# Ternary weights transposed by DMA, level scores without a rounded split, and new instruction lists in a one-core level tower

## The reference

```python
h = level_emb[levels] * 0.15
h = h + attention(layernorm(h))        # 16 query heads, 4 key heads of 16, softmax over all 128 tokens
def _quantize(W):                      # W1: 1024 x 256, W2: 256 x 1024
    gamma = jnp.mean(jnp.abs(W))
    return jnp.clip(jnp.round(W / (gamma + EPS)), -1.0, 1.0)
h = h + relu(layernorm(h) @ _quantize(W1).T + b1) @ _quantize(W2).T + b2
```

## Time and profile before

| | us |
|---|---|
| median of 3 runs (lowest, highest) | 53.73 (53.23, 56.08) |
| the profiled execution: time | 54.04 |
| the profiled execution: span | 52.0 |
| PE busy | 45.6 (88%) |
| PE weight loads | 36.3 (70%) |
| DVE busy | 38.0 (73%) |
| ACT busy | 34.2 (66%) |
| POOL busy | 15.7 (30%) |

### The profile page before, as it was taken

The page is one execution under the profiler, slowest core; times in us unless marked ns, Lnnn a source line. Parts: engine busy times, 40 slices in busy tenths (PEclk is TensorE's granted clock), DMA queues, the critical chain, the costliest instruction groups (busy, mean ns, idle before and its releaser), DMA issues.

```text
span 52.0 us, 1206 instructions
## 1 busy us (share of the span) xinstructions
PE 45.6 (88%) x394; PEld 36.3 (70%) x394; DVE 38.0 (73%) x141; ACT 34.2 (66%) x77; POOL 15.7 (30%) x37
## 2 busy tenths in 40 slices
PE   0999999999999799999999999999999999993000
PEld 0336469894758688768679999989999798860000
DVE  3558994698985289999999996269858889659100
ACT  0083231380799997989988999999967793509000
POOL 5689952000005950009200579970000000000000
PEclk9999999999999999999999999999999999999997
DMA  0183919999753100000000000000000005555893
GB/s 0 36 234 77 44 63 350 410 432 368 198 124 98 47 7 0 0 0 0 0 0 13 0 0 0 0 6 0 0 0 0 0 13 200 203 208 195 295 385 127
DMA packets 4658, 5.37 MB, mean 103 GB/s; under 512 B 1117, under 2 KB 4141, under 8 KB 4653
## 3 DMA queue, kind: packets, MB, share of 16 engines
q1 hardware_dynamic: 4312, 5.02, 31.2%
q10 hardware_dynamic: 341, 0.29, 1.6%
HBM read 3.21 MB, written 2.10 MB: 102 GB/s over the span
## 4 chain that ended last, share of the span: by engine, by line
PE 76%; DVE 10%; POOL 3%; issue 1%; ACT 1%; DVEq 1%
PE pswt L1258 16%; PE psmisc L1273 15%; PE psg L1067 8%; PE psg L1063 5%; PE psg L1194 4%; POOL rs L445 3%; PE psg L1240 3%; DVE aw L952 2%; PE psg L1106 2%; PE psg L1153 2%; PE psg L1203 2%; PE psg L1154 2%; PE psg L1158 2%; DVE cn L892 2%; DVE hq L906 2%; DVE st L910 2%
## 5 line engine op out<-in xcount | busy, mean ns | idle before, releaser
L587 ACT ACTIVATE hr<-pswt,b1c 128x256 f32<-128x256 f32 x16 | 7.6, 484 | 1.2 <-PE pswt L1258 0.9
L1273 PE MATMUL psmisc<-w2T,hh 128*128 128x256 f32 x32 | 8.2, 285 | 0.0
L1273 PE MATMUL psmisc<-w2T,hl 128*128 128x256 f32 x32 | 8.1, 281 | 0.0
L937 DVE TENSOR_TENSOR hl<-hr,hh 128x256 fp32r<-128x256 f32 x16 | 6.7, 435 | 1.2 <-ACT hh L589 0.9
L1258 PE MATMUL pswt<-xhi,w1T 128*128 128x256 f32 x32 | 7.0, 299 | 0.0
L1258 PE MATMUL pswt<-xlo,w1T 128*128 128x256 f32 x32 | 6.4, 280 | 0.0
L1273 PEld LDWEIGHTS psmisc<-w2T,hh 128*128 128x128 f32 x32 | 6.0, 189 | 0.1
L1273 PEld LDWEIGHTS psmisc<-w2T,hl 128*128 128x128 f32 x32 | 6.0, 189 | 0.0
L445 POOL TENSOR_TENSOR rs<-ve,mhalf 128x1 f32<-128x1 f32 x4 | 2.7, 686 | 9.1 <-DVE ve L918 9.1
L440 POOL TENSOR_TENSOR voc<-vo,cpos 128x272 f32<-128x272 f32 x4 | 2.7, 714 | 8.1 <-DVE cpos L858 8.1
L1258 PEld LDWEIGHTS pswt<-xhi,w1T 128*128 128x128 f32 x32 | 4.9, 189 | 0.3
(11 more groups left out here) (177 smaller groups left out, 108.4 us busy)
## 6 DMA issues: line engine op xcount, KB each, us to landing
w<-in_L_ffn_W_dram SPq DMA_DIRECT2D x4, 512.0 KB, 6.8
out_dram<-aw SPq DMA_DIRECT2D x7, 256.0 KB, 2.4
wq<-in_L_attn_Wq_dram SPq DMA_DIRECT2D x1, 256.0 KB, 3.5
wo<-in_L_attn_Wo_dram SPq DMA_DIRECT2D x4, 64.0 KB
out_dram<-aw ACTq DMA_DIRECT2D x1, 256.0 KB, 2.9
emb<-in_L_tok_level_emb_dram SPq DMA_DIRECT2D x1, 128.0 KB
bo_bc<-in_L_attn_bo_dram SPq DMA_DIRECT2D x1, 128.0 KB, 8.8
b_bc<-in_L_ffn_b_dram SPq DMA_DIRECT2D x1, 128.0 KB, 7.3
```

What stands on the lines that cost most here:

```text
L587: nc.scalar.activation(hr[:, n % NHR, :], pswt[n % 2][:, 0:RH], ACT.Relu, bias=b1c[:, j:j + 1]).then_inc(a_hr, 1)
L937: V.tensor_tensor(hl[:, n, :], hr[:, n % NHR, :], hh[:, n, :].bitcast(F32), ALU.subtract).then_inc(v_hl, 1)
L1273: ins = mm(psmisc[r][:, 0:D], part[:, n, r * P:(r + 1) * P], w2T[:, j, :], start=(j == 0 and m == 0), stop=(j == FC - 1 and m == 1))
```

## The change

- **DMA-transposed weights.** Both matrices are made ternary in the same way on ACT (`rounded(w, i)`, `ternary(w, i)` for w = 0, 1). SP issues four DMA transposes of a 128 x 1024 bf16 half each, one per finished `ternary`. POOL copies the result in eight pieces of 128 x 512 from bf16 to the matmul's type (`weights_in`). PE's `weights_t`, ACT's `weights_out`, DVE's `signs` and `ternary` and the two bf16 identities are gone. The sums of absolute values of W2 move from ACT to DVE (a reduction over 1024 columns, twice).
- **Scores.** No split: keys and queries stay f32, the 64 rows of a head pair go into 64 partitions twice, so that matmuls use half of the array's rows. Groups 0 and 1 get one f32 matmul of 512 columns each, with the lower and with the upper 64 rows. Groups 2 and 3 get none: PE writes only mask and maximum, and DVE adds the score table `st` (`arguments`, 128 x 512, PSUM to SBUF) before ACT's exp. The masks are four matmuls of 32 rows.
- **Loads.** W1 is loaded third, by rows of 1 KB; `wk`, `wv`, `bk` go to the ACT queue, and the tokens come in three DMAs. `b1` is gathered element by element.
- **Stores.** ACT copies sequences 0 and 2 of a group, DVE 1 and 3; a pair's store waits for one copy of each.
- **Lists.** All five lists are written anew.

```diff
-            sp.dma_start(b1c[:], b1.rearrange("(p j) -> p j", j=FC)).then_inc(d_b1, 16)
+            sp.dma_start(b1c[:], b1.rearrange("(j p) -> p j", p=P), allow_slow_non_contiguous=True).then_inc(d_b1, 16)
             sp.dma_start(b2_bc[:], ...)
+            for w in range(2):
+                for i in range(2):
+                    sp.wait_ge(a_tern, 2 * w + i + 1)
+                    sp.dma_start_transpose(wT[:, w, FC * i:FC * i + FC, :], tern[:, w, 1024 * i:1024 * i + 1024]).then_inc(d_wt[2 * w + i], 16)
...
+            def weights_in(u):                                  # POOL
+                w, q = divmod(u, FC // 2)
+                pool.wait_ge(d_wt[u // 2], 16)
+                src = wT[:, w, 4 * q:4 * q + 4, :].rearrange("p (j k) f -> p j k f", k=KC)
+                if w == 0:
+                    nc.gpsimd.tensor_copy(w1T[:, 2 * q:2 * q + 2], src).then_inc(g_wt, 1)
+                else:
+                    nc.gpsimd.tensor_copy(w2T[:, 2 * q:2 * q + 2, :].rearrange("p j (k f) -> p j k f", k=KC), src).then_inc(g_wt, 1)
...
             inverse_root(0)                                     # POOL's list
             inverse_root(1)
+            weights_in(0)
+            weights_in(1)
+            weights_in(2)
+            weights_in(3)
+            weights_in(4)
             inverse_root(2)
+            scaled_mean(2)
+            weights_in(5)
             inverse_root(3)
-            scaled_mean(2)
             scaled_mean(3)
-            residual(0)
             residual(1)
+            weights_in(6)
             residual(2)
+            weights_in(7)
             residual(3)
...
             exps(0)                                             # ACT's list, from the first exp on
             exps(1)
             exps(2)
-            rounded(0)
+            rounded(0, 0)
+            rounded(0, 1)
             ctx_out(0)
             ctx_out(1)
             exps(3)
-            rounded(1)
-            ternary(0)
+            ternary(0, 0)
+            ternary(0, 1)
             ctx_out(2)
-            ternary(1)
-            weights_out(0)
+            rounded(1, 0)
+            ternary(1, 0)
             ctx_out(3)
             x_hi(0)
-            weights_out(1)
             x_hi(1)
-            weights_out(2)
-            weights_out(3)
-            weights_out(4)
+            rounded(1, 1)
             hidden(0, 0)
             hidden(0, 1)
-            weights_out(5)
+            ternary(1, 1)
             hidden(0, 2)
...
+            def query_out(i):                                   # DVE; ACT has the other half of the columns
+                dve.wait_ge(p_q, 1)
+                V.tensor_copy(qs[64 * i:64 * i + 64, :].rearrange("p (a e l) -> p a e l", a=2, e=2)[:, :, 1, :],
+                              psg[3][64:P, 0:2 * L].rearrange("p (a l) -> p a l", a=2)).then_inc(v_q, 1)
+            def arguments(g):                                   # DVE, groups 2 and 3
+                dve.wait_ge(p_et, 1)
+                dve.wait_ge(a_st, 1)
+                V.tensor_tensor(et[:, g], st[:].unsqueeze(1).to_broadcast([P, BG, P]), psg[g][:, :].rearrange("p (b n) -> p b n", b=BG),
+                                ALU.add).then_inc(v_arg, 1)
+            def magnitudes(i):                                  # DVE
+                dve.wait_ge(d_w2[i], 16)
+                V.tensor_reduce(asum[:, 2 + i:3 + i], w2[:, i, :], AX_X, ALU.add, apply_absolute_value=True).then_inc(v_abs, 1)
...
-            def scores_t(g):
-                rhs = qs[:].unsqueeze(1).to_broadcast([P, BG, P])
-                mm(psg[g][:, :], khi[:], rhs, start=True, stop=False)
-                mm(psg[g][:, :], klo[:], rhs, start=False, stop=False)
-                mm(psg[g][:, :], gone[:], seln[:, g * BG:(g + 1) * BG]..., start=False, stop=True)
+            def scores_t(*gs):
+                for g in gs:
+                    h = slice(64 * (g % 2), 64 * (g % 2) + 64)
+                    mm(psg[g][:, :], ktm[h, :], qs[h, :].unsqueeze(1).to_broadcast([64, BG, P]), start=True, stop=False, skip_group_check=True)
+            def masks():
+                for g in range(NG):
+                    q = slice(L * g, L * (g + 1))
+                    mm(psg[g][:, :], gone[q, :], seln[q, :].unsqueeze(2).to_broadcast([L, BG, P]), start=g in SUBTRACTED, ...)
...
             queries()                                           # PE's list, up to the first context
-            keep_warm(5, psg[0])
             values()
             scores()
-            scores_t(0)
-            levels_out()
+            score_table()
+            scores_t(0, 1)
             level_ends()
             prefix_t()
-            scores_t(1)
+            keep_warm(4, psg[3])
+            counts()
+            keep_warm(1, psg[3])
             maxima()
-            scores_t(2)
-            scores_t(3)
-            counts()
+            masks()
+            keep_warm(4, psmisc[0])
             less_max()
```

More of the change, by code:

```diff
@@ L293, in level_tower @@
         a_abs = sem("a_abs")
-        v_sgn = sem("v_sgn")
+        v_abs = sem("v_abs")
         p_gam = [sem(f"p_gam{i}") for i in range(2)]
         v_thr = sem("v_thr")
-        v_tern = sem("v_tern")
-        p_wt = sem("p_wt")
-        a_wt = sem("a_wt")
+        d_wt = [sem(f"d_wt_{i}") for i in range(4)]
+        g_wt = sem("g_wt")
         p_f1 = sem("p_f1")
@@ L524, in max_hi @@
                 nc.scalar.activation(mhi[:], psmisc[1][:, 0:P], ACT.Copy).then_inc(a_mhi, 1)
[L526 to L533, removed]
-                act.wait_ge(c_magic, 2)
-                c = slice(1024 * q, 1024 * q + 1024)
-                src = w1[:].rearrange("p j d -> p (j d)")[:, c]
-                nc.scalar.activation(aw[:, 0, c], src, ACT.Identity, bias=magic[:, 0:1], scale=inv[:, 0:1]).then_inc(a_rnd, 1)
@@ new lines, in rounded @@
+            def rounded(w, i):
+                if w == 0:
+                    act.wait_ge(a_abs, 2)
+                act.wait_ge(v_inv, w + 1)
+                act.wait_ge(c_magic, 2)
+                js = slice(FC // 2 * i, FC // 2 * (i + 1))
+                y = aw[:, w, 1024 * i:1024 * i + 1024]
+                if w == 0:
+                    nc.scalar.activation(y, w1[:, js, :].rearrange("p j d -> p (j d)"), ACT.Identity,
+                                         bias=magic[:, 0:1], scale=inv[:, 0:1]).then_inc(a_rnd, 1)
+                else:
+                    nc.scalar.activation(y.rearrange("p (j k f) -> p j k f", k=KC, f=P),
+                                         w2[:].rearrange("p k (j f) -> p j k f", f=P)[:, js], ACT.Identity,
+                                         bias=magic[:, 0:1], scale=inv[:, 1:2]).then_inc(a_rnd, 1)
@@ L974, in _ @@
[L974 to L989 removed]
+            spread_selectors()
+            level_scan()
+            level_ends()
+            end_codes()
@@ L990, in _ @@
+            key_blocks()
+            end_columns()
+            level_onehot(0)
+            query_out(0)
+            query_out(1)
+            level_onehot(1)
+            prefix_max(0)
+            values()
+            count_blocks()
+            prefix_max(1)
+            mask_selectors()
+            top_onehot()
+            gone_levels()
+            low_rows()
+            counts_out()
             max_parts()
-            count_blocks()
-            counts_out()
-            signs(1)
+            arguments(2)
@@ L994, in _ @@
             threshold(0)
+            arguments(3)
             inverse_sums(0)
+            table_bias()
+            inverse_sums(1)
             normalise(0)
-            inverse_sums(1)
             normalise(1)
+            magnitudes(0)
+            magnitudes(1)
             inverse_sums(2)
+            add_table(0)
             normalise(2)
-            table_bias()
+            row_stats(0)
             threshold(1)
-            ternary(0)
-            add_table(0)
-            row_stats(0)
+            row_moments(0)
@@ L1006, in _ @@
             add_table(1)
-            row_moments(0)
+            variance_eps(0)
             row_stats(1)
             inverse_sums(3)
-            variance_eps(0)
             row_moments(1)
+            variance_eps(1)
+            norm_rows(0)
             normalise(3)
-            variance_eps(1)
-            ternary(1)
-            norm_rows(0)
             norm_rows(1)
-            ternary(2)
-            ternary(3)
+            add_table(2)
             x_lo(0)
             x_lo(1)
-            add_table(2)
+            row_stats(2)
```

406 lines of the change are left out of this document (167 added, 239 removed).

## The result

| | before | changed kernel |
|---|---|---|
| median of the runs | 53.68 us (53.23 to 56.08, 4 runs) | 61.05 us (60.42 to 61.95, 4 runs) |
| ratio, 95% interval | 1 | 1.1283 [1.1183, 1.1383] |
| profiled execution: time, span, mean granted clock | 54.04, 52.0, 0.995 | 60.42, 58.5, 0.89 |

What follows compares the result with a forecast made beforehand. ScalarE's list, with TensorE and VectorE close behind, sets the FFN's start, and TensorE runs the FFN. Profiled 54.04 - 0.1 (up to the last spread) - 0.2 (tail) = 53.7, or 53.4 us on the median's scale; range 52.0 to 55.8.

Steps and rivals of the forecast that it cites:

- the front: Stretch up to the first exp: queries 0.9 later, scores 0.35 later, yet first exp at 16.3, a gain of 0.5.
- the condition: Front: the forecast is wrong if queries or tokens come over 0.5 us later than predicted, since nothing behind recovers it.
- First exp: End of the front: starts at 16.3 instead of 16.83, a gain of 0.5, with less_max near 15.5 instead of 15.81.
- First exp to FFN: ScalarE's list up to x_hi(1) grows from 9.76 to 10.75; FFN starts at 27.7 instead of 28.00, gain 0.3.
- Transposes: Weight transposes by DMA before POOL's copies: each lands after 3.0 us, bounds 2.4 and 6.8.
- rivals 2 and 4: FFN: transposes land late (55.0 us at 5 us each, chance 0.19) or queue up (68 to 69 us, chance 0.04).
- rival 2: FFN's first half: transposes land late, the third delaying ffn2(0, 0); 55.0 us if 5 us each; chance 0.19.
- POOL copies: Copies of transposed weights on POOL: 0.75 us per 128 x 512 piece, bounds 0.4 and 2.0.
- rival 3: POOL copies cost 1.2 us a piece, so ffn1(1, 0) moves by 2: 55.4 us; chance 0.09.
- First half of the FFN: ffn1(1, 0) at 35.95, 0.85 later, TensorE idling 1.1 us; twelve ffn2 done instead of eight, worth 0.95.
- rival 1: FFN's first half: the 1.1 us of idle TensorE are not there, so 52.3 us; chance 0.30.
- Tail: Last stores: the pair before the last is ready 0.4 earlier; gain 0.2, bounds 0 and 0.4.

Runs made afterwards that it cites:

- e1: The changed kernel, all of it, but with both load lists of the kernel before: 54.18 us, ratio 1.0107.
- e7: e1 with ctx_out(0), ctx_out(1) and exps(3) ahead of rounded(0, 1) on ScalarE, and table_bias and W2's second sum later on VectorE: 54.33 us, ratio 1.0115.
- e9: e1 without the twelve filler matmuls between table_t and the queries: 54.67 us, ratio 1.0128.
- e6: The changed kernel with 25 fillers instead of 3 where TensorE waits for bq: 61.15 us.
- e8: e1 with all four groups' scores written by TensorE, none added on VectorE, and five fillers left out: 54.17 us, ratio 1.0082.
- e3: The changed kernel with W1 issued on SP only when bk has landed, bv standing behind that wait: 58.01 us, ratio 1.0814.
- e5: As e3, but with bv issued ahead of SP's wait for bk: 58.29 us, ratio 1.0806.
- e4: The kernel before with the change's two new load lists and nothing else: 63.03 us, ratio 1.1785.
- e2: The changed kernel with bk and bq issued ahead of wk and wv on ScalarE's queue: 64.95 us, ratio 1.2086.

## Why the prediction was wrong, step by step

**The step that failed.** It is the front: "which also wait for the second weight copy on ScalarE, behind seven DMA issues instead of two: queries end near 10.75". I priced the issues and never the landings. I let the small loads land as they did before while 2 MB were issued ahead of or beside them, and the early issue of W1 does not stand in the sum at all. The queries ended at 14.63. With the loads of before they end at 10.15 in e1 and 10.67 in e7, at or ahead of my figure, so the rest of the step was sound. I named the condition myself: the forecast is wrong "if queries or tokens come over 0.5 us later than I have them". Tokens came 1.8 later than before (5.90 against 4.12), and I gave the condition no price and no rival.

The price was in the trace of before. Its DMA issues hold three small loads that are issued behind the weights:

```profile
bo_bc<-in_L_attn_bo_dram SPq DMA_DIRECT2D x1, 128.0 KB, 8.8
b_bc<-in_L_ffn_b_dram SPq DMA_DIRECT2D x1, 128.0 KB, 7.3
...
b1c<-in_L_ffn_b_dram SPq DMA_DIRECT2D x1, 4.0 KB, 7.6
```

A 4 KB load lands after 7.6 us there, and 64 KB issued ahead of the weights after 3.2. As an estimate, those rows bound the landing of a small load between 3 and 8.8 us, and by the dear end `bq`, issued at 3.31, comes at 12.1. Its matmul stood at 8.40 before, so that is 3.7 us on the chain and a rival at 57.1, the clock not yet counted.

**The clock, which no term held.** I had all stretches at full clock, because the trace of before shows nothing else. Of the 7.41 us, 2.14 and 2.20 are work of TensorE at half clock. The second amount came again in e9, with the loads in time (2.08); the first was not measured apart. The fillers that the change adds stand before and behind the wait for `bq` and not in it.

**First exp.** Predicted 16.3; with the loads as before 15.80 in e1 and 16.34 in e7, whose lists are the same up to there: a gain of 1.03 and of 0.49 where I said 0.5. `less_max` starts at 15.08 and 15.62, where I had 15.5. The front's arithmetic was right in mechanism; that one profile hits it to 0.04 is luck, as two profiles of the same front differ by 0.5.

**First exp to FFN.** Predicted 11.4, measured 11.12 in the changed kernel and 11.77 in e1. The parts: `arguments` 0.687 (0.70); reductions 1.210 (1.15, bounds 0.7 and 1.3); in e1 VectorE's list waits for `bo` until 18.39, 0.85 us that I did not have. FFN start 27.57 in e1 (27.7); by the timeline it was 27.80 before, so the gain there is 0.2.

**Transposes.** Predicted 3.0 (bounds 2.4 and 6.8), measured 2.8; rivals 2 and 4 did not come about, save one step of rival 2 in e1, below; in e6, without a reason that the runs show, they took 2.8 to 5.0 and TensorE waited 0.7 us for `w1T`. The Trainium skill's page Advanced Engine Details and Errata (X-Bar Transpose) has them as fast as ordinary DMAs, and the rows agree nearly (a store of the same 256 KB lands after 2.3). The Trainium skill's page DMA: Bandwidth & Descriptors (the part on the fast DGE) has one push per tile for earlier generations. An issue takes 1.2 to 1.3 us here, against 0.4 to 0.7 for most single loads; whether that price is in it no run shows.

```profile
wT<-tern SPq DMA_TRANSPOSE x4, 2.8
```

**POOL copies.** Predicted 0.75 (0.4 and 2.0), measured 0.63 for W1 and 0.75 for W2; rival 3 fell.

```profile
L451 POOL CAST w2T<-wT 128x512 fp32r<-128x512 bf16 x4 | 3.0, 746 | 1.2 <-DMA wT<-tern 1.2
...
L449 POOL CAST w1T<-wT 128x512 fp32r<-128x512 bf16 x4 | 2.4, 627 | 0.1
```

**First half of the FFN.** Predicted `ffn1(1, 0)` 8.25 us behind the start; 8.33 in the changed kernel (34.33 to 42.66), 8.27 in e8, 8.89 in e1. In e1 the fourth transpose was issued for 2.71 us and landed 4.1 later, so POOL's seventh copy began at 34.51 and TensorE waited until 35.27: the step of rival 2, worth 0.6. Why that issue was long stays open; e8 issued its own at the same 30.34, in 1.23. FFN start to last spread: predicted 19.05, measured 19.15. So the stretch is as long as I said and rival 1, by which it would be 1.1 shorter, fell. The 1.1 us of idle TensorE that I named as the reason are not in the profile as such: it counts TensorE busy for 8.14 of the 8.33 us, and its busy time is modelled and overlaps. The gain of the front is gone there: `ffn1(1, 0)` starts at 36.46 in e1 and 35.86 in e8 against 35.09 before, and the four further `ffn2` done by then are worth 0.95, which leaves e1 0.42 behind and e8 0.18 ahead.

**Tail.** Predicted a gain of 0.2; from the end of the last spread to the end 7.19 before (46.85 to 54.04), 6.94 now (53.48 to 60.42), 7.12 in e1 and 7.03 in e8: gains of 0.25, 0.07 and 0.16, inside the bounds.

**The sum with that one step repaired** is e1, measured at 54.18, where I had said 53.4: inside the range, but 1% slower than before and not 0.6% faster. Its profiled execution (54.38) is 0.64 above my sum of 53.74: the first exp 0.50 early, then 0.37 late to the FFN, 0.64 in the FFN's first half, nothing in its second, 0.13 in the tail. That the total is this near is in part luck, since the errors cancel. My chance of 0.32 for slower lay wholly on transposes and copies, and neither was slow.

## What to carry to other kernels

Before a large load is moved ahead of small ones, price the landing of every load that is issued beside or behind it, from a row where a small load already shares the engines with a large one, and follow who waits for it. Where TensorE would idle for it, price the work that follows at the lower clock as well: here that was more than half of the lateness of the first exp. A wait taken away at one load moves to the next in the list (`bk`, then `bv`, then `bo`), so move the small ones together.

## What the runs showed of the hardware

- A load of 64 KB on ScalarE's queue landed 2.2 to 2.5 us after its issue with the weights held back (e3, e5), 5.9 to 8.9 beside them (changed kernel, e4, e6), and 10.7 and 11.1 in e2; a queue of its own did not protect it. In two profiled executions with the same load lists (changed kernel and e6) the use of `wk`, `bq` and `bk` differed by 1.4 to 1.6 us.
- An issue can take its engine's queue for long. The 128 KB of `b2`, issued right behind `b1`, took SP 3.45 to 5.02 us in the eleven kernels that gather `b1` element by element, and 1.20 and 0.56 in the kernel before and in e4, which load `b1` in runs of eight. That the gather does it fits all thirteen, but no run changes it alone.
- The granted clock fell to half after TensorE had been busy for 1.55 of 3.50 us, but also in e9, where TensorE counts as busy for 3.44 of the 3.50 us before, with small matmuls and no fillers; in e1, with twelve fillers more, it did not fall. Idle time alone is thus not what decides; what does stays open here.
- A cast on VectorE of 128 x 256 takes 287 ns on average before and 473 in the changed kernel: 0.29 for each of five there, and 0.62 to 0.75 for the four (35.59, 37.45, 40.05, 42.21) that begin beside a POOL cast or addition of 256 columns or more (from 35.58, 37.07, 39.90, 42.06); one at 36.71, beside one-column work on POOL, took 0.29. That the two engines slow each other is argued from this alone, and was not tried.
